# Closing the program's block without GpSimd's drain

## The reference, cut to what matters

```python
h = _layernorm(x) * (1 + ca) + sa
x = x + ga * attention(h)            # 16 heads, second-order Taylor features, causal
h = _layernorm(x) * (1 + cb) + sb
x = x + gb * experts(h)

# experts: 8 of them, each takes the 512 tokens with the highest probability
route_prob = softmax(h @ Ws + bs).T                    # 8 x 4096
route_vals, routes = top_k(route_prob, 512)            # 8 x 512
out = (gelu(h[routes] @ W1 + b1) @ W2 + b2) * route_vals[..., None]
final = zeros.at[routes].add(out)                      # scatter with addition
```

## Time and profile before

| | |
|---|---|
| median of 3 runs | 352.97 us (352.78 to 354.15) |
| profiled execution, its own time | 356.2 us |
| its span, first to last instruction | 354.5 us |
| start of the last scatter | 345.35 us |
| busy share | PE 69%, DVE 59%, POOL 50%, PEld 49%, ACT 46% |

### The profile page before, as it was taken

How to read it: one execution, slowest core, us unless ns; L and a number is a source line. 1 busy time by engine, 2 the same in 40 slices (tenths; PEclk the granted TensorE clock), 3 DMA queues, 4 the chain that set the end, 5 groups by cost and what they waited for, 6 DMA issues and landing times.

```text
span 354.5 us, 8066 instructions
## 1 busy us (share of the span) xinstructions
PE 246.0 (69%) x3056; PEld 174.3 (49%) x3056; DVE 210.8 (59%) x675; ACT 162.3 (46%) x223; POOL 177.3 (50%) x221
## 2 busy tenths in 40 slices
PE   1689989999999999999743411226899966976000
PEld 1346657676676767777522300113566663764000
DVE  4164898989898999979784588694042302212100
ACT  5267758786867858686500365102133403202000
POOL 5507347373646637350615000047557887777661
PEclk9999999999999999999995565555999988789555
DMA  7607201010101001010113999924313433442321
GB/s 216 172 3 281 81 17 47 17 47 9 40 15 30 30 15 44 18 48 18 32 30 58 89 99 275 251 41 111 96 16 76 59 56 76 65 49 24 30 22 15
DMA packets 30542, 24.06 MB, mean 68 GB/s; under 512 B 6368, under 2 KB 27184, under 8 KB 30128
## 3 DMA queue, kind: packets, MB, share of 16 engines
q0 software_dynamic: 6848, 9.06, 18.0%
q1 hardware_dynamic: 23664, 14.59, 13.8%
HBM read 15.11 MB, written 8.54 MB: 67 GB/s over the span
## 4 chain that ended last, share of the span: by engine, by line
DVE 32%; POOL 24%; issue 14%; PE 13%; DMA 6%; ACT 5%; another core or an unknown queue 2%; DVEq 1%; SPq 0%; POOLq 0%; ACTq 0%
POOL out_y L570 13%; POOL rstd L481 3%; POOL area L560 3%; ACT area L703 3%; DVE y_s L785 3%; DMA modb<-mod_rows 3%; DMA out_y<-o_sb,idx 3%; DVE low L1058 2%; DVE y_n L790 2%; PE ps L1145 2%; DVE xn L825 2%; DVE area L750 2%; DVE wgt L760 2%; POOL vare L479 2%
## 5 line engine op out<-in xcount | busy, mean ns | idle before, releaser
L634 ACT ACTIVATE wgt<-ps 128x1024 f32<-128x1024 f32 x64 | 62.3, 1028 | 37.0 <-PE ps L1145 37.0
L570 POOL DMA_INDIRECT out_y<-o_sb,idx x32 | 50.7, 1583 | 21.2 <-issue 8.5
L560 POOL DMA_INDIRECT area<-token_rows,idx x32 | 31.0, 969 | 52.0 <-DVE idx L1071 42.5
L1145 PEld LDWEIGHTS ps<-area 32*128 32x128 f32 x1024 | 42.1, 184 | 24.8 <-ACT wgt L644 13.9
L1145 PE MATMUL ps<-area 32*128 32x64 f32 (+3 forms) x1024 | 50.2, 321 | 2.9 <-ACT wgt L634 1.2
L714 ACT ACTIVATE area<-ps,b_sb 128x512 f32<-128x512 f32 x32 | 21.4, 687 | 53.8 <-PE ps L1347 53.5
L1175 PE MATMUL ps<-wgt,v_bd 128*32 128x259 f32 (+3 forms) x1024 | 42.0, 304 | 3.8 <-DVE y_t L776 3.1
L1357 PE MATMUL ps<-modb,area 128*128 128x128 f32 x256 | 35.3, 304 | 2.5 <-ACT area L714 2.5
L1357 PEld LDWEIGHTS ps<-modb,area 128*128 128x128 f32 x256 | 34.3, 219 | 4.3 <-ACT area L714 4.3
L1175 PEld LDWEIGHTS ps<-wgt,v_bd 128*32 128x32 f32 x1024 | 29.0, 109 | 14.9 <-DVE y_t L776 4.4
L1347 PE MATMUL ps<-area,xall 128*128 128x512 f32 x64 | 31.5, 626 | 2.4 <-issue 1.3
(11 more groups left out here) (181 smaller groups left out, 441.9 us busy)
## 6 DMA issues: line engine op xcount, KB each, us to landing
modb<-mod_rows SPq DMA_DIRECT2D x3, 1024.0 KB, 7.5
out_y<-x SPq DMA_DIRECT2D x16, 128.0 KB, 1.8
token_rows<-h SPq DMA_DIRECT2D x16, 128.0 KB, 1.9
token_rows<-gb_mod POOLq DMA_DIRECT2D x1, 2048.0 KB, 28.1
xall<-in_w SPq DMA_DIRECT2D x1, 2048.0 KB, 28.7
modb<-in_w SPq DMA_DIRECT2D x8, 256.0 KB, 6.4
xall<-in_x SPq DMA_DIRECT2D x2, 768.0 KB, 8.0
xall<-in_x SPq DMA_DIRECT2D x2, 256.0 KB, 4.4
```

What stands on the lines that cost most here:

```text
L560: eng.indirect_dma_start(out=xg[e % 4][:, j, :], out_offset=None, in_=rows[:, :], in_offset=bass.IndirectOffsetOnAxis(ap=idx[:, e, j:j + 1 ...
L570: eng.indirect_dma_start(out=out[:, :], out_offset=bass.IndirectOffsetOnAxis(ap=idx[:, e, j:j + 1].bitcast(u32), axis=0), in_=o_sb[e % 2][ ...
L634: k = nc.scalar.activation(wgt[bb][:, 2 * half:2 * half + 2, :, 0:256], ps[:, 2 * half:2 * half + 2, :].rearrange("p c (a q) -> p c a q", ...
L1145: return mm(ps[:, cc, col:col + SEQ - key * BK], k_bd[par][qd][r, 4 * bb + key, :, :].rearrange("p a k -> p (a k)"), q_sb[par][qd][r, t0 + ...
```

## The change

The block is opened with a flag. With it, closing the block puts no DRAIN into GpSimd's queue. The other four engines keep theirs, and so does the handshake. The waits inside GpSimd's function, that of line 586 among them, are not touched.

```diff
--- before.py
+++ after.py
@@ -339,7 +339,7 @@
 
             eng.sem_inc(s_turn, 1)
 
-        block = ctx.enter_context(nc.Block())
+        block = ctx.enter_context(nc.Block(no_gpsimd_drain=True))
```

## The result

The changed kernel takes 347.47 us (median of 4 runs, 346.78 to 348.37), the kernel before 353.20 us (4 runs, 352.78 to 354.15, three of them those of the table of times). The ratio is 0.9832, with a 95% interval of 0.9805 to 0.986: 1.4 to 1.95% faster, 5.7 us by the medians. The forecast was 347.5 us.

The account below looks back on a forecast made before the run. GpSimd was taken to set the end, its last scatter landing followed by a serial DRAIN. The median of 352.97 us less 5.46 us gave 347.5 us, range 346.7 to 351.2 us.

Parts of the forecast that it names:

- The whole DRAIN counts: At the block's end, GpSimd's 5,416 ns DRAIN is covered by nothing; with the handover, removing it saves 5.46 us.
- Nothing takes its place: At the block's exit, other engines' DRAINs are over by 330.6 us; the handshake still takes 0.25 us.
- Nothing comes back behind the span: In the closing part after the span, an undrained GpSimd adds 0 to 0.17 us, at most 5.42.
- Rival 1: Behind the span, the closing part's first drain pays the 5.42 us; time stays 352.97 us; chance 0.12 whole.
- as a share: Behind the span, the closing part pays only part of the DRAIN's time: 348 to 351.2 us; chance 0.08.
- Rival 2: At the block's exit, the handshake needs GpSimd's DRAIN, so the long one stays: 352.97 us; chance 0.03.
- Rival 3: The DMA list is gone through at the closing and again at the next opening: 358.4 us; chance 0.05.
- the two hypotheses on what the DRAIN does: GpSimd's end DRAIN either goes through 67 DMAs at 78 ns each or has a fixed cost after any DMA.

Follow-up runs that it names:

- e7: The changed kernel run once more, on another chip beside the kernel before: 347.38 us, 0.9837 of the kernel before.
- e1: The changed kernel plus a hand-written drain on GpSimd behind the wait for the last scatters: 356.99 us, 1.0001 of the kernel before.
- e2: The changed kernel plus a `dma_reset()` on GpSimd behind the wait for the last scatters: 351.10 us, 0.9837 of the kernel before.
- e6: The changed kernel plus 32 stores of 16 bytes issued by GpSimd ahead of the gathers: 355.43 us, 1.0071 of the kernel before.
- e9 to e11: The changed kernel plus 16 stores of 16 bytes, 64, or 32 with a hand drain behind their landing: 357.62, 365.98 and 360.09 us.
- e5: The kernel before plus 32 stores of 16 bytes issued by GpSimd ahead of the gathers: 362.66 us, 1.0266 of the kernel before.
- e4: The kernel before plus one more GpSimd drain ahead of the first scatter: 355.21 us, 0.9951 of the kernel before.
- e3: The kernel before without the wait of line 586 for the last scatters: 354.65 us, 0.9939 of the kernel before.
- e8: The kernel before without line 586, plus drains ahead of the scatters of experts 0, 5, 6 and 7: 351.20 us, 0.9946.

## Why the prediction was right

**The whole DRAIN counts.** Predicted 5.46 us, from the DRAIN's start to POOLq's next instruction. Shown: 5.4 us less between the same two instructions, 5.7 us by the first medians (4.9 to 6.9 by the interval) and 5.4 us in e7. e1 puts the drain back and has all of it again. The mechanism is the predicted one. That the median fell within 0.1 us of the forecast is luck: the four runs of after lie 1.6 us apart, and the median of before stood at 352.97 us when the forecast was made and at 353.20 us in the comparison.

**Nothing takes its place.** Predicted: the other DRAINs are over, the handshake takes as long as before, the wait for the last scatters is next. The rows of after show all three: from POOLq's first semaphore instruction to the end of the span it is 0.2 us before (354.3 to 354.5) and after (345.4 to 345.6). The prediction took the saving for a constant and not for a share of the time. e7 and e2 (5.4 and 5.6 us, where the kernel before took 352.8 and 356.7 us) can't tell one from the other. What supports a constant is the DRAIN's length: 5,416 ns in the kernel before and in e1, and otherwise by the number of DMAs.

**Nothing comes back behind the span.** This was the open step, with 0 to 0.17 us taken and 5.42 as the bound. The distance of span and time is 1.67 to 1.78 us in all four runs of after, as in the 26 recorded ones of before in the sets of the experiments, and e6 and e9 to e11 show that it doesn't depend on the list. Rival 1 falls, whole and as a share. The reason that I gave, that a part which only resets state needs no count of old transfers, is supported by e2 (296 ns for a reset behind the same DMAs), but no row shows the closing part itself, so as its cause it is argued.

By the Trainium skill's "Runtime: NRT & Kernel Launch", section on the preamble and postamble, a barrier behind the kernel waits for all engines. No row of this case shows that barrier; the unchanged 1.7 us say only that the undrained DMAs added nothing to whatever stands there. By the Trainium skill's "VectorE: DVE Perf Modes", section "The DRAIN you can't avoid", the DRAINs there take some 12 ns each. No row shows them either; the 1.7 us leave room for 12 ns on GpSimd and exclude 5.4 us.

**Rival 2** (the flag does nothing, the handshake needs the DRAIN) falls by the rows of line 68. **Rival 3** (the list is met again at the next opening) falls by the time: it asked for 358.4 us, and the slowest run of after took 348.37 us. Which kernel ran ahead of each run isn't recorded, but no run of any kernel with or without the flag stands 5 us above its fellows. The opening of the profiled execution shows nothing that grew either; its DRAIN takes the 169 ns of the earlier trace rows:

```profile
L1385 POOLq DRAIN  x1: 169/169/169, 0.4 to 0.4; - x1
```

**What was not predicted.** The span was to be 349.0 us, with the stretch up to the last scatter unchanged. It came out at 345.6, and that stretch was 3.4 us shorter: VectorE's late start in the first expert of the profile before, which has nothing to do with the flag. The prediction took the whole span of one profile as the base for the span of another. Had I read the drop of the spans alone as the effect, I would have overstated it by some 60%. The reading of the two hypotheses on what the DRAIN does, 78 ns for each DMA or a fixed price, was left open in the prediction; the five lengths settle it at 79 ns a DMA with 160 ns fixed.

## What to carry to other kernels

Look at what ends the program behind the last landing: a stretch in which every engine and the DMA share read 0.00 is serial time, and a DRAIN on GpSimd in it cost about 80 ns for each DMA that GpSimd had issued since its last one. Where the program waits for all of these DMAs by semaphore, as this one does, it can be left out; nothing in these runs needed it. Where a drain must stay, leave out the wait ahead of it (2.0 us here), or drain earlier, where GpSimd waits for longer than its list is worth and its DMAs have landed. And compare two profiles stretch by stretch before giving the difference of their spans to the change.

## What was unexpected of the hardware

- The DRAIN of GpSimd takes time in proportion to the DMAs that it issued, 79 ns each, with all of them landed. Their bytes are of no account: 82 ns for a store of 16 bytes (e5), 76 ns on average for 16 gathers and the three plain DMAs, the largest of 2 MB (e4). The DRAIN of `dma_reset()` took 296 ns for 67.
- The bar of a DRAIN on POOLq isn't its cost. It may begin well ahead of the end of the engine's earlier work: 11.4 us in e3, of which 5.4 us lay behind the last issue, and 15.6 us ahead of the first scatter in e8, which came 1.5 us later for it.
- 32 DMAs of 16 bytes on GpSimd's queue, in its idle time, made the kernel with the flag 8.0 us slower (355.43 against 347.38 us), most of it through a store on SyncE's queue that went out 6.2 us later.
- On two of the three chips VectorE began its work on the first expert's output 2.8 to 4.1 us behind the matmuls that it waits for, and on the third at once. The medians of the kernel before differ by as much (356.7 and 356.1 against 352.8 us). Its cause wasn't found.
- Time behind the span went from 1.7 to 2.2 us in two kernels and back to 1.7 in a longer one. What sets it wasn't found.
